# Where the split of the edge weights is made: ahead of the first window spans, by ScalarE and GpSimd in turn

## What is computed

```
edge_index = [src, dst]
h = relu(layernorm(x)); x = x + L0(h)   # three hops of D^-1/2 A D^-1/2, mean of the four terms
h = relu(layernorm(x)); x = x + L1(h)   # GCN: deg = segment_sum([edge_weight, 1], [dst, self]), relu
h = relu(layernorm(x)); x = x + L2(h)   # h W_self + mean of the neighbours W_neigh
h = relu(layernorm(x)); x = x + L3(h)   # message and node MLPs over the edges
```

## Time and profile before

| | before |
|---|---|
| median of 3 runs | 1075.51 us (1074.43 to 1076.52) |
| the profiled execution | 1078.87 us, its span 1077.1 us |
| PE, DVE, ACT, POOL busy, share of the span | 86%, 77%, 42%, 53% |
| mean granted clock of PE | 0.92 of full speed |

### The profile page before, as it was taken

The page is one execution under the profiler, slowest core; times in us unless marked ns, Lnnn a source line. Parts: engine busy times, 40 slices in busy tenths (PEclk is TensorE's granted clock), DMA queues, the critical chain, the costliest instruction groups (busy, mean ns, idle before and its releaser), DMA issues.

```text
span 1077.1 us, 23987 instructions
## 1 busy us (share of the span) xinstructions
PE 921.8 (86%) x6195; PEld 584.2 (54%) x6195; DVE 827.8 (77%) x2585; ACT 450.3 (42%) x879; POOL 574.0 (53%) x747
## 2 busy tenths in 40 slices
PE   3788888699977777877789859999999999999995
PEld 2466665355535556666565535555555555555563
DVE  8988888743569788898876776777777787777776
ACT  2577777310005454544421234444434434434431
POOL 6533433000015777777710067777777777777770
PEclk9677777899988999999889969999999999999997
DMA  3000000610002111111126165544544545445441
GB/s 66 2 1 0 0 0 0 229 70 1 1 0 47 26 26 27 27 26 27 27 87 189 27 173 116 115 103 107 108 101 104 109 98 105 109 100 105 102 92 33
DMA packets 144600, 72.30 MB, mean 67 GB/s; under 512 B 111661, under 2 KB 136442, under 8 KB 144410
## 3 DMA queue, kind: packets, MB, share of 16 engines
q1 hardware_dynamic: 127224, 54.98, 19.5%
q0 software_dynamic: 15936, 16.35, 8.6%
q10 hardware_dynamic: 1378, 0.22, 0.1%
HBM read 59.13 MB, written 12.35 MB: 66 GB/s over the span
## 4 chain that ended last, share of the span: by engine, by line
PE 44%; DVE 21%; POOL 13%; issue 10%; ACT 5%; DMA 4%; DVEq 2%; ACTq 1%; SPq 1%; POOLq 0%
PE seg L1627 9%; POOL A L1221 7%; POOL pair L1221 6%; PE seg L1812 6%; PE big L1848 5%; PE big L1557 5%; ACT A L1356 4%; DVE A L1974 3%; PE big L1838 3%; PE seg L1859 3%; PE seg L1880 3%; PE seg L1571 2%; DMA A<-table,src_i 1%; DVE A L1963 1%; DVE acc_mem L1985 1%
## 5 line engine op out<-in xcount | busy, mean ns | idle before, releaser
L1221 POOL DMA_INDIRECT A<-table,src_i x338 | 323.1, 956 | 114.7 <-issue 97.5
L1221 POOL DMA_INDIRECT pair<-table,src_i x160 | 162.2, 1013 | 62.1 <-issue 48.5
L1356 ACT CAST A<-big 128x500 f32 x208 | 125.4, 603 | 48.1 <-PE big L1562 26.8
L1812 PE MATMUL seg<-A 128*128 128x384 f16 (+1 forms) x624 | 121.4, 338 | 11.9 <-DVE A L2040 8.2
L1471 ACT COPY A<-big 128x512 f32<-128x512 f32 x104 | 60.8, 584 | 121.3 <-PE big L1838 119.7
L1848 PE MATMUL big<-A 128*128 128x512 f32 x208 | 109.8, 610 | 0.5 <-DMA A<-pr_table 0.5
L1477 ACT ACTIVATE A<-big,A 128x512 f32<-128x512 f32 x104 | 71.5, 688 | 92.0 <-PE big L1849 92.0
L1671 PE MATMUL big<-A 128*128 128x300 bf16 (+1 forms) x512 | 93.8, 328 | 16.5 <-DVE A L1963 15.7
L1812 PEld LDWEIGHTS seg<-A 128*128 128x128 f16 x624 | 57.4, 99 | 91.2 <-issue 36.7
L1284 POOL COPY cur<-pair 128x24 bf16 x100 | 40.2, 446 | 94.6 <-PE seg L1571 94.6
L2074 DVE TENSOR_TENSOR A<-seg,A 128x448 f32<-128x448 f32 x78 | 48.7, 624 | 47.5 <-PE seg L1815 29.6
(11 more groups left out here) (321 smaller groups left out, 1734.2 us busy)
## 6 DMA issues: line engine op xcount, KB each, us to landing
A<-in_edge_attr_dram SPq DMA_DIRECT2D x103, 128.0 KB
A<-drel_flat SPq DMA_DIRECT2D x104, 126.0 KB
spilled_adjacency<-A SPq DMA_DIRECT2D x1, 7074.0 KB, 21.8
A<-spilled_adjacency SPq DMA_DIRECT2D x6, 1152.0 KB, 9.9
A<-table,src_i POOLq DMA_INDIRECT x338
A<-pr_table SPq DMA_DIRECT2D x104, 31.5 KB
pair<-table,src_i POOLq DMA_INDIRECT x160
A<-low_flat SPq DMA_DIRECT2D x78, 32.0 KB, 3.1
```

The source lines that it names most:

```text
L1221: pool.indirect_dma_start(out=row, out_offset=None, in_=table, in_offset=bass.IndirectOffsetOnAxis(ap=src_i[:, tile:tile + 1], axis=0)).th ...
L1356: nc.scalar.copy(A[:, :, bass.ds(bases[k], PW)], big[:, k % 4, 0:PC].rearrange("p (s d) -> p s d", d=PW)).then_inc(window_kept, 1)
L1812: op = nc.tensor.matmul(made[:, 0:held.shape[2] * D], hot_low[:, u, m, :], held[:, k, :, :], start=(m == 0 and k == 0), stop=(m == 3 and k ...
```

## The change

The split no longer stands between the clearing of A's edges and the iota on POOL. PE turns `raw_w` first of all rows, and counts it on `cols_ps`. ACT copies `wcol` out of PSUM ahead of `low_16`, and makes the three casts to bf16, at four places between its other copies; POOL makes only the two subtractions, between its memsets of `w_parts` and the centring. Each step waits for the other engine's step before (`w_rounded` counts the casts, `w_left` the subtractions). ACT no longer waits for `w_parts_ready` ahead of its copy of `src_i` at the end of the window stage. DVE waits for `cols_ps` of 5 rather than 4.

```diff
@@ -1250,6 +1250,11 @@
                                ALU.subtract).then_inc(ev("drel_t_ready"), 1)
             pool.memset(w_parts[:, T:TK, :], 0.0)
             pool.memset(w_parts[:, 0:T, 0], 1.0)
+            pool.wait_ge(ev("w_rounded"), 1)
+            pool.tensor_tensor(w_res, wcol[:, 0:T], w_parts[:, 0:T, 1], ALU.subtract).then_inc(ev("w_left"), 1)
+            pool.wait_ge(ev("w_left"), 1)
+            pool.wait_ge(ev("w_rounded"), 2)
+            pool.tensor_tensor(w_res, w_res, w_parts[:, 0:T, 2], ALU.subtract).then_inc(ev("w_left"), 1)
             pool.wait_ge(ev("mean0_ready"), 1)
             pool.tensor_tensor(total, xs[:, :, :], per_node(st_c), ALU.subtract).then_inc(ev("centred0"), 1)
             pool.wait_ge(ev("keys_ready"), 1)
@@ -1259,15 +1264,7 @@
             pool.memset(A[:, :, N - PW:AW], 0.0).then_inc(ev("edges_cleared"), 1)
 
 
-            pool.wait_ge(ev("edge_cols"), 2)
-            pool_link(pool.tensor_copy(w_parts[:, 0:T, 1], wcol[:, 0:T]))
-            pool_link(pool.tensor_tensor(w_res, wcol[:, 0:T], w_parts[:, 0:T, 1], ALU.subtract))
-            pool_link(pool.tensor_copy(w_parts[:, 0:T, 2], w_res))
-            pool_link(pool.tensor_tensor(w_res, w_res, w_parts[:, 0:T, 2], ALU.subtract))
-            pool_link(pool.tensor_copy(w_parts[:, 0:T, 3], w_res))
-            pool.sem_inc(ev("w_parts_ready"), 1)
-
-
+            pool.wait_ge(ev("w_rounded"), 3)
             pool.wait_ge(ev("ranges_ready"), 1)
 
             pool.wait_ge(ev("variances0"), 1)
@@ -1338,11 +1335,18 @@
             act.wait_ge(ev("src_lo_ready"), 1)
             nc.scalar.copy(key_l_t, src_lo).then_inc(ev("key_l_t_ready"), 1)
             nc.scalar.copy(src_t, raw_src).then_inc(ev("src_t_ready"), 1)
+            act.wait_ge(ev("cols_ps"), 1)
+            nc.scalar.copy(wcol[:, :], banks[6][:, 0:TK]).then_inc(ev("edge_cols"), 1)
+            act.wait_ge(ev("edge_cols"), 1)
+            nc.scalar.copy(w_parts[:, 0:T, 1], wcol[:, 0:T]).then_inc(ev("w_rounded"), 1)
             act.wait_ge(ev("src_low_ready"), 1)
             nc.scalar.copy(low_16, src_low).then_inc(ev("rows_16_ready"), 1)
-            for n, b, t in ((5, 4, drel[:, :]), (6, 6, wcol[:, :])):
-                act.wait_ge(ev("cols_ps"), n)
-                nc.scalar.copy(t, banks[b][:, 0:TK]).then_inc(ev("edge_cols"), 1)
+            act.wait_ge(ev("w_left"), 1)
+            nc.scalar.copy(w_parts[:, 0:T, 2], w_res).then_inc(ev("w_rounded"), 1)
+            act.wait_ge(ev("cols_ps"), 6)
+            nc.scalar.copy(drel[:, :], banks[4][:, 0:TK]).then_inc(ev("edge_cols"), 1)
+            act.wait_ge(ev("w_left"), 2)
+            nc.scalar.copy(w_parts[:, 0:T, 3], w_res).then_inc(ev("w_rounded"), 1)
             act.wait_ge(ev("w2_ps"), 1)
             nc.scalar.copy(w2_t[:, :], banks[7][:, 0:D]).then_inc(ev("edge_cols"), 1)
             act.wait_ge(ev("centred0"), 1)
@@ -1363,7 +1367,6 @@
             with act.Fori(1, ITB) as it:
                 keep_windows(it, True)
 
-            act.wait_ge(ev("w_parts_ready"), 1)
             nc.scalar.copy(src_i[:, :], banks[5][:, 0:TK]).then_inc(ev("src_kept"), 1)
 
             def copy_turned2(place):
@@ -1514,6 +1517,10 @@
                     op = nc.tensor.transpose(banks[b][:, c * P:(c + 1) * P], t[:, c * P:(c + 1) * P], ident[:, :])
                 op.then_inc(ev("cols_ps"), 1)
 
+            pe.wait_ge(ld_edges, 13 * 16)
+            for c in range(4):
+                op = nc.tensor.transpose(banks[6][:, c * P:(c + 1) * P], raw_w[:, c * P:(c + 1) * P], ident[:, :])
+            op.then_inc(ev("cols_ps"), 1)
             turn_rows0(0, dst_t, "dst_t")
             turn_rows0(1, key_r_t, "key_r_t")
             turn_rows0(2, key_l_t, "key_l_t")
@@ -1523,9 +1530,6 @@
                 op = nc.tensor.matmul(banks[7][0:1, P:P + THR], ones[:, :], below[:, c * THR:(c + 1) * THR], start=(c == 0), stop=(c == 3))
             op.then_inc(ev("counts_ps"), 1)
             turn_rows0(4, drel_t, "drel_t")
-            for c in range(4):
-                op = nc.tensor.transpose(banks[6][:, c * P:(c + 1) * P], raw_w[:, c * P:(c + 1) * P], ident[:, :])
-            op.then_inc(ev("cols_ps"), 1)
             turn_rows0(5, src_t, "src_t")
             pe.wait_ge(ld_w, 16 * 5)
             pe.wait_ge(ev("ranges_ready"), 1)
@@ -2132,7 +2136,7 @@
             link(dve.tensor_reduce(st_a[:, :], xs[:, :, :], AX.X, ALU.add))
             dve.tensor_scalar(st_c[:, :], st_a[:, :], 1.0 / D, None, ALU.mult).then_inc(ev("mean0_ready"), 1)
 
-            dve.wait_ge(ev("cols_ps"), 4)
+            dve.wait_ge(ev("cols_ps"), 5)
             dve.tensor_copy(key_r, banks[1][:, 0:TK])
             dve.tensor_copy(key_l, banks[2][:, 0:T])
             dve.memset(key_b[:, 0:1], NO_KEY)
```

## The result

| | before | after |
|---|---|---|
| median of 8 runs | 1076.63 us (1074.43 to 1079.58) | 1070.23 us (1066.9 to 1072.42) |
| ratio, 95% interval | | 0.9936, 0.9922 to 0.9951 |
| profiled execution, its span | 1078.87, 1077.1 us | 1069.76, 1068.0 us |

The ratio of 0.9936, which compares the means of the runs, makes 6.9 us of 1076.63; the two medians lie 6.4 apart. In the changed kernel the lines of PE's, DVE's and ScalarE's window stage are four higher (the degree sums L1571 are L1575), those of POOL's iota and key distances three lower (L1274 is L1271).

What follows compares the result with a forecast made beforehand. The prediction took DVE, held up by POOL's split before the window loop, as the bound: 3.83 us saved less 0.87 for a subtraction gives 2.96, from median 1075.51 to 1072.5 us. The 8-in-10 range was 1070.9 to 1075.7.

Steps and rivals of the forecast that it cites:

- What bounds the opening stretch: 24.29 to 34.59 us: DVE's hots, lanes and boundary lanes held up by POOL's split; removing it saves 3.83 us.
- Windows 0 to 3 as the next limit: Second eight hots on DVE wait until these windows are built; they stay at 1.77 us, with cover of 0.5.
- PE, POOL's idle time: Keys turned about 0.8 us later on PE, covered by 0.7; subtractions fit POOL's idle time, centring at most 0.1 later.
- What the subtractions hold up: On DVE: the first subtraction costs the compares 0.87 us; the second falls under the reduction and costs 0.
- The sum of the opening stretch: Before the window loop: 3.83 saved less 0.87 held up on DVE, 2.96 us.
- nothing on the path, 0: ACT's casts, at most 0.62 us each, and its copy of wcol fit its queue off the path; cost 0.
- the front costs nothing: Rival: subtraction 1 finds DVE first, so the whole 3.83 us is saved, 1071.7 us; chance 0.11.
- The two about the loop: Window loop gives the lead back, about 1074.9 us (0.23 together with DVE not freed), or falls into a slower rhythm, 1078.6 (0.09).
- three signs of being wrong: Iota later than 33 us; reduction L2132 stretched; or iota early but the end of the window stage not.

Runs made afterwards that it cites:

- f1: The kernel before with three one-element copies on ScalarE ahead of its window loop, nothing else changed; 1072.79 us, ratio 0.9958.
- e4: The changed kernel with each POOL subtraction begun when a DVE reduction begins, and the third cast behind ScalarE's copies of turn 0; 1069.92 us, ratio 0.9931.
- e1 to e3: Changed kernel with two idle DVE reductions ahead of turn 0 (1072.46 us), the same with one (1070.58), and the kernel before without the split (1072.59).
- g3: The changed kernel with the copies of drel and w2_t on DVE instead of ScalarE; 1075.98 us, ratio 0.9979.

## Why the prediction was right in direction and wrong in size

- *What bounds the opening stretch:* right. DVE held up by the split, instruction by instruction; 3.91 came off where 3.83 was worked out.
- *Windows 0 to 3 as the next limit:* right, the second eight hots kept their 1.77.
- *PE, POOL's idle time:* right that none is on the path, wrong in two times. The keys were turned at 19.12 (15.75 + 3.37) and not at 19.9, so no cover was needed. The centring began at 21.82, 1.07 later than before where 0.1 at most was forecast, behind subtraction 2 and behind the mean, which DVE had at 21.74.
- *What the subtractions hold up:* 0.85 for the 0.87 taken, in part by luck: the 0.87 was from an instruction of another kind, and subtraction 1 began at 18.23, not 17.8. For the second, 0.23 and not 0: the reduction was indeed not held, but casts of 1.12 in place of 0.62 brought the subtraction onto the multiply behind it.
- *The sum of the opening stretch:* 2.96 forecast, 2.82 in the trace.
- *ScalarE, "nothing on the path, 0":* this is the step that failed. As work the casts did cost nothing. But each of them also moves all that follows in ScalarE's program by one instruction, and with three the window loop left a place where each turn takes 0.155 longer (f1: the same from three idle copies). The step left as it was at 6.40 was in truth a term of the sum, of 24 x 0.155 = 3.7 us, nearly as large as the 3.83 for the whole split. With it the sum would have been 2.96 + 3.7 = 6.7, and the time 1068.8 from the median shown, or 1069.9 from the median of 8.
- *The rivals:* "the front costs nothing" came out true of e4 alone. The two about the loop had the right place, but looked for a rhythm set by its beginning, which e1 to e3 rule out, and expected only loss. Of the three signs of being wrong none came up, since none looked at the step of the loop.

**What stays open.** Why ScalarE's sequencer takes 0.09 more ahead of instruction 47, and 0.06 more behind the branch, when the loop begins at 44 to 46. No row shows what it waits for there. Whether ScalarE's program has more such places, or the loops of the other engines or of the last layer have them, was not tried. Nor are the differences between single executions behind 200 us explained.

## What to carry to other kernels

Side work on POOL is not hidden where it makes DVE stand still: look for pairs of instructions whose ends coincide, and put the side work under a reduction, which here never stood still. When a loop that was not touched changes its step, compare the idle time at its turn on each engine before looking for a cause in the data flow. And before a saving of a few microseconds is put down to an edit, time the old kernel with as many idle instructions added on the same engine: here three such copies gave 4.5 us, and the edit without the gift of the loop (g3) 2.3, with intervals that overlap.

## What the runs showed of the hardware

- The idle time of ScalarE at the turn of a loop of 35 instructions is 0.695 or 0.54 us, depending on where the loop lies in its program, by as little as one instruction (46 against 47), and by nothing else that was tried. 0.09 of the difference stands at one place in the program, ahead of instruction 47, whichever instruction of the loop that is.
- The Trainium skill, in "SBUF — State Buffer", section "Who interferes with whom", has a reduction never contend with GpSimd on trn2, and a copy, cast or TENSOR_SCALAR in a two-port mode stand still for the whole of a GpSimd instruction that was issued first. The runs agree: reductions kept their 1.81 us beside subtractions (e4), and a compare that began 0.04 behind a subtraction of 1.08 took 1.11 where the shortest took 0.26.
- A cast on ScalarE of 128 x 416 from f32 to bf16 with a stride of four values took 1.12 us, where one of 128 x 512 in dense rows to f16 took 0.62.
